# An upper bound for the indices of every gather of node rows in a graph attention layer

## The reference

```python
h = jnp.maximum(_layernorm(x, axis=-1), 0.0)
h_edge = ((h[src] + bond) @ W).reshape(-1, H, D)
el = jnp.einsum('ehd,hd->eh', h_edge, attn_l)
er = jnp.einsum('nhd,hd->nh', (h @ W).reshape(-1, H, D), attn_r)
s = el + er[dst]
s = jnp.where(s > 0, s, NEG_SLOPE * s)
ex = jnp.exp(s - jax.ops.segment_max(s, dst)[dst])
alpha = ex / jax.ops.segment_sum(ex, dst)[dst]
ft = jax.ops.segment_sum(h_edge * alpha[..., None], dst)
out = x + relu(batch_norm(ft.mean(axis=1)) * gamma + beta)
```

## Time and profile before

| | us |
|---|---|
| time, median of 2 runs | 2341.9 (2339.57 to 2344.23) |
| span of the profiled execution | 2008.4 |
| median less that span | 333.5 |
| POOL busy | 1485.0 |
| DVE busy | 1131.0 |
| PE busy | 926.1 |
| PEld busy | 662.6 |
| ACT busy | 114.1 |

### The profile page before, as it was taken

How to read it: one execution, slowest core, us unless ns; L and a number is a source line. 1 busy time by engine, 2 the same in 40 slices (tenths; PEclk the granted TensorE clock), 3 DMA queues, 4 the chain that set the end, 5 groups by cost and what they waited for, 6 DMA issues and landing times.

```text
span 2008.4 us, 19568 instructions
## 1 busy us (share of the span) xinstructions
PE 926.1 (46%) x6252; PEld 662.6 (33%) x6252; DVE 1131.0 (56%) x3243; ACT 114.1 (6%) x239; POOL 1485.0 (74%) x1579
## 2 busy tenths in 40 slices
PE   3537545434443454344435543544355335534455
PEld 2425333323332332233323322332233223322245
DVE  7878656545554555455545554555455546554565
ACT  3410000000000000000000000000000000000002
POOL 7777777777777777777777777777777777777771
PEclk9758767666776676667766666666666666666676
DMA  8734322322232223222322232223222322232234
GB/s 232 182 70 124 92 59 60 81 70 60 60 85 66 60 60 91 60 59 60 92 60 59 60 92 59 59 60 92 59 60 60 91 60 60 60 91 60 60 69 133
DMA packets 73591, 157.09 MB, mean 78 GB/s; under 512 B 29092, under 2 KB 33712, under 8 KB 66832
## 3 DMA queue, kind: packets, MB, share of 16 engines
q0 software_dynamic: 50208, 53.02, 15.7%
q1 hardware_dynamic: 22162, 99.02, 14.9%
q10 hardware_dynamic: 1112, 3.73, 0.7%
HBM read 144.42 MB, written 9.80 MB: 77 GB/s over the span
## 4 chain that ended last, share of the span: by engine, by line
POOL 67%; issue 22%; DVE 4%; PE 3%; DMA 2%; ACT 0%; ACTq 0%; DVEq 0%; SPq 0%; POOLq 0%
POOL work L696 67%; PE p_s L944 1%; DMA er_run<-er_tab,er_idx 1%; DMA h_tab<-acc 1%; DMA acc<-in_x 1%; PE po L1082 1%; PE pt L933 0%; POOL er_run L710 0%; DVE acc L1261 0%; DVE acc L1259 0%; DVE acc L1569 0%; DVE work L1253 0%; DVE scaled L1251 0%; PE pt L1142 0%; DVE ohT_i L1363 0%
## 5 line engine op out<-in xcount | busy, mean ns | idle before, releaser
L696 POOL DMA_INDIRECT work<-h_tab,srcI x1498 | 1414.0, 944 | 456.5 <-issue 456.2
L1209 DVE COPY elh<-work 128x16 f32<-128x16 f32 x196 | 39.0, 199 | 731.9 <-DMA work<-h_tab,srcI 729.1
L1019 PE MATMUL p_s<-ident,elh 128*32 128x128 f32 x196 | 50.6, 411 | 769.6 <-DVE elh L1209 769.6
L1082 PE MATMUL po<-scaled,work 128*65 128x64 f32 x3104 | 250.0, 257 | 77.8 <-issue 74.8
L1019 PEld LDWEIGHTS p_s<-ident,elh 128*32 128x32 f32 x196 | 25.7, 155 | 780.9 <-DVE elh L1209 777.0
L1082 PEld LDWEIGHTS po<-scaled,work 128*65 128x65 f32 x3104 | 244.6, 173 | 88.1 <-issue 87.2
L982 PE MATMUL p_s<-work,wpair 128*32 128x256 f32 x784 | 235.8, 468 | 15.6 <-DVE p_r L1487 14.0
L969 PE MATMUL pt<-ident,work 128*128 128x128 f32 x784 | 158.2, 353 | 60.6 <-DVE work L1214 59.8
L1569 DVE TENSOR_TENSOR acc<-acc,po 65x64 f32 x776 | 168.3, 217 | 28.8 <-DVE acc L1569 2.7
L969 PEld LDWEIGHTS pt<-ident,work 128*128 128x128 f32 x784 | 124.1, 183 | 89.4 <-DVE work L1214 84.6
L982 PEld LDWEIGHTS p_s<-work,wpair 128*32 128x32 f32 x784 | 100.6, 134 | 146.0 <-issue 68.1
(11 more groups left out here) (212 smaller groups left out, 945.6 us busy)
## 6 DMA issues: line engine op xcount, KB each, us to landing
work<-in_ea_t SPq DMA_DIRECT2D x49, 1024.0 KB, 6.4
ohT_i<-in_dst_n SPq DMA_DIRECT2D x49, 512.0 KB, 3.4
work<-h_tab,srcI POOLq DMA_INDIRECT x1498, 2.5
acc<-hT_tab SPq DMA_DIRECT2D x2, 1562.5 KB, 14.4
h_tab<-acc SPq DMA_DIRECT2D x1, 2887.5 KB
work<-in_x SPq DMA_DIRECT2D x1, 2800.0 KB
out<-work SPq DMA_DIRECT2D x5, 448.0 KB
acc<-in_x ACTq DMA_DIRECT2D x3, 672.0 KB
```

The lines of the kernel that those rows point to most:

```text
L696: pool.indirect_dma_start(out=row, out_offset=None, in_=x if c < RAW else h_tab, in_offset=bass.IndirectOffsetOnAxis(ap=srcI[:, c, j, g:g ...
L1019: m = mm(sT_ps[:, j * P:(j + 1) * P], elh[:, c % 2, j, :, :].rearrange("p h g -> p (h g)"), ident[:, :], start=False, stop=True, skip_grou ...
L1082: m = mm(bank[0:F1, w0:w0 + H * WIN], edge[c % 2][:, j, g, :], scaled[:, j * CG + g, :, :].rearrange("p h w -> p (h w)"), start=(j == 0), ...
```

## The change

Each gather of line 696 gets an upper bound for its index, `bounds_check=N - 1` (12499), and `oob_is_err=False`: a row whose index is above the bound is left out of the transfer without an error. No index is above it, so all rows are still fetched.

```diff
                     row = gat[q][:, j, g, 0:F] if c < RAW else gat[q][:, j, g, :]
                     pool.indirect_dma_start(out=row, out_offset=None, in_=x if c < RAW else h_tab,
-                                            in_offset=bass.IndirectOffsetOnAxis(ap=srcI[:, c, j, g:g + 1], axis=0)
-                                            ).then_inc(gat_in[q][k], 16)
+                                            in_offset=bass.IndirectOffsetOnAxis(ap=srcI[:, c, j, g:g + 1], axis=0),
+                                            bounds_check=N - 1, oob_is_err=False).then_inc(gat_in[q][k], 16)
```

## The result

| | before | after |
|---|---|---|
| time, median of 2 runs, us | 2341.9 (2339.57 to 2344.23) | 2433.05 (2426.47 to 2439.62) |
| span of the profiled execution, us | 2008.4 | 2423.7, in an execution of 2426.5 |

The changed kernel is slower: ratio of the times 1.0394, with a 95% interval of 1.0352 to 1.0436. The 2433.05 us lie inside the predicted range of 2335 to 2500 us. The likeliest case, no change at 2345.0 us, did not come; the side that the prediction gave 0.43 did.

A forecast was written before the change was run, and what follows sets the result against it. The prediction took POOL, saturated with gathers at a fixed pitch, as the bound. The 2008.4 us span plus 3.1 us for the test gave 2011.5; with the same 333.5 us around it, 2345.0 us, range 2335 to 2500.

The forecast's parts named there:

- the side that the prediction gave 0.43: Whole kernel: slower by over 2%, made up of rival A, C and the rest of Rival B; chance 0.43.
- what bounds the kernel in the profile shown: POOL, saturated with gathers at a fixed pitch of 1.249 us; all other engines have time to spare.
- the 333.5 us around the span: Median time of before less its 2008.4 us profiled span; carried unchanged into the forecast time.
- no cover exists for a slower gather: POOL's gathers: a nanosecond on the pitch costs 1562 ns; 30.0 ns a gather makes 2%.
- the MOVE at 0: POOL's sequencer: each 29 ns MOVE is hidden behind the gather before it, costing 0; without the cover 45.3 us.
- Rival B: POOL's sequencer: the MOVE isn't hidden and enters the 305 ns ahead of each gather; 45.3 us, 2387 us; chance 0.08.
- C: POOL's register: its MOVE waits for queued gathers, each dispatched only after the one before; 250 us, 2592 us; chance 0.06.
- the wait that moves, at 0: POOL's gathers: the MOVE takes the wait, but no semaphore comes less than a dispatch ahead; 0, bound 60 us.
- the test, at 2 ns: Making of the transfers' addresses in each gather: 2 ns more, 3.1 us in all; upper bound 95 ns, 148.4 us.
- rival A: Gathers' address making: the test costs on each row; half the row's work is 47 ns, 2416 us; chance 0.34.
- The prediction's mark for A: POOL's gathers at line 696: a mean over 974 ns at an unchanged gap.
- The mark for the sequencer: POOL's sequencer: its wait of line 706 still more than 10 us ahead, as a sign that the forecast is right.

The follow-up runs named there:

- e7: The changed kernel (bound and MOVE on each gather) without POOL's waits for PE from chunk 5 on; 2098.71 us, ratio 1.0446 to the kernel before.
- e1: The kernel before, unedited, profiled again at the long level (the slower of its two levels of time); 2341.7 us, ratio 0.9988.
- e4: The changed kernel with each MOVE placed ahead of the waits, so that these stay on the gathers; 2352.7 us, ratio 1.0053 to the kernel before.
- e3: The kernel before plus a MOVE ahead of each of the 1562 gathers, taking over the waits; only the last gather bounded; 2406.7 us, ratio 1.0269.
- e8: The kernel before with the `er_run` gathers changed: 128 rows and fewer, some bounded, the 1562 gathers left unbounded; one run, 2030.04 us.

## Why the prediction was right and wrong

- **Right: what bounds the kernel in the profile shown.** At the short level POOL's pitch is the time: e7's 86.1 us more of gathers gave 86.7 us more of span.
- **Wrong: the 333.5 us around the span.** There are 2.8 us around it in the execution after and 2.0 in e1. The profile and the times of before belonged to two levels, and the prediction carried the difference over as a constant. At the level that was timed, POOL is not saturated: it stands after nearly each 16 gathers, for counts of PE that come 10.7 and 14.2 us late in e1. That the device time was 17% above the span should have been the first question; "no cover exists for a slower gather" was then read from the one execution and held for all.
- **Right: the MOVE at 0.** 1562 MOVEs with the waits left on the gathers (e4), and 1562 of them at the short level (e7), cost nothing that shows. Rival B fell, and so did C: the "issue" ahead of a gather is 0.30 us in e7 and in the kernel after.
- **Wrong: the wait that moves, at 0.** The mechanism was named, that the MOVE takes the wait and the sequencer stands, and so was the condition, that a semaphore comes less than a dispatch ahead of its gather. What failed is the claim that this never happens, read from the earlier trace rows. At the long level it happens 95 times in e3 and 75 times in the kernel after, and each start is 0.52 us later, not the 0.16 us taken as the dispatch. By e3 and e4 the whole is 65 to 80 us, over the bound of 60 us and the larger part of the 91 us; 49 and 39 us of it are these later starts, if they count in full, and the rest stays open.
- **Wrong in size: the test, at 2 ns.** It measured 53 ns, within the bounds of 0 and 95 ns and near the half-way case of rival A (47 ns). But A's reason fell as well, since the cost doesn't go by rows (e8). The rows that showed "forms alike" differed in table and width, and in nothing that the test touches.
- **The sum that comes out.** At the long level: 11 us for the test, 65 for the waits, and 15 more when both are there, 91 us on 2341.8. The ratio of 1.039 is near what the test alone gives at the short level (1.043 to 1.045) by coincidence. Rival A's 2416 us would have been close for a reason that is mostly not the one at work. That the time fell into the predicted range is thus luck in good part: the upper end of 2500 us was set by a test that costs by rows, and it took in a loss that came mostly from the moved waits.
- **What would show it.** The prediction's mark for A, a mean over 974 ns, came. The mark for the sequencer, line 706 passed more than 10 us ahead, did not come and did not tell: the sequencer passed it at 93.6 us after and at 93.3 in e1, 3.65 and 2.55 us ahead of the next gather, so it moved with the level and not with the change. None of the marks would have caught the moved waits; the idle time of POOL with a releaser does.

No version beat both kernels. If the bound is wanted, e4's order gives it for 11 us at the long level.

## What to carry to other kernels

Compare the span of the profile with the time that was measured before anything else; where they are 300 us apart, the profile is of another execution than the runs, and its "saturated" engine may have slack in them. When an edit puts a register move between a wait and the instruction that it was for, the wait moves to the register move, and every start that is really held comes one dispatch later, here 0.52 us; write the move ahead of the wait. A longer instruction on an engine that is being held can cost less than its own length, where it takes something out of the stall, here 11 us instead of 83.

## What was not expected of the hardware

- An indirect gather of 128 rows takes 944 ns of POOL without a bound and 997 ns with one, and 16 rows take 861 and 909 ns: about 50 ns for the bound at either size.
- A held gather starts 258 ns after the semaphore's count if it carries the wait itself, and 777 to 780 ns after it if a MOVE ahead of it does.
- With either placing POOL's sequencer stands: the next MOVE comes 32 ns behind the count where the gather carries the wait (e4), and the MOVE that carries it comes 23 ns behind (e3).
- The same program took 2009 us in some sets of runs and 2342 to 2350 us in others, on one chip too. The difference in the traces is on PE. Its count of `p_turned` comes 10.7 us behind the matmul that makes it in e1 (median), and 0.01 us in the profile of before, and its next instruction comes late 0 times or some 400 times, in steps of about 0.7 us, while DVE and ACT show no such gaps. In the kernel after 426 of the 485 late ones come while POOL's sequencer executes no MOVE for over 1.6 us, so stands, and it stands so for 1498 of 2376 us. In e4, with the waits on the gathers, it is 363 of 402, and 1425 of 2301 us. Whether POOL's standing makes PE late or PE's lateness makes POOL stand was not settled.
